# Four conditional layers on one core: the early expert blocks ordered by hand, their sums on two other engines, and two units of layer 3 moved

## The chip, the cores and the metric

One core of one Trainium2 chip. The time is the device time of one launch in microseconds (us). The engines are TensorE (PE, its weight loads shown as PEld), VectorE (DVE), ScalarE (ACT), GpSimd (POOL) and SyncE (SP); each runs its own instructions in order and waits on semaphores for the others.

## The reference, cut to what matters

Input x is 16 samples of 128 tokens by 128 columns. Each of four layers picks its weights by an index per sample or per token:

```python
# layer 0: one of 8 feed-forward networks per sample, then a layer norm
h = gelu(x @ Wi[i0] + bi[i0]); x = layernorm(h @ Wo[i0] + bo[i0] + x) * g[i0] + b[i0]
# layer 1: norm per token, norm over the tokens of a sample, scale and shift by a small network
h = norm_tokens(norm(x) * ln_g + ln_b) * gamma + beta
gates, idx = top_k(softmax(h @ router_w), 2)          # 2 of 8 experts per token
x = x + sum_over_the_two(gate * (relu(h @ w1[e] + b1[e]) @ w2[e] + b2[e]))
# layer 2: pairs of columns rotated by an angle per sample
# layer 3: down to 32 columns, gelu, a 32x32 expert per sample, up again, residual, layer norm
a = gelu(x @ down_W.T + down_b)
x = layernorm((a @ expert_W[i3].T + expert_b[i3] + emb[i3]) @ up_W.T + up_b + x) * g3 + b3
```

## The kernel before, in words

Layer 0 runs sample by sample on PE (`up`, `down`), in four groups of four samples. Groups 0 and 1 (half 0) are carried through layer 1's norm and router while groups 2 and 3 are still in layer 0.

Layer 1's experts work on blocks of 128 token rows that share an expert; there are NBLK = 39. A block's rows are fetched from a DRAM copy of h by an indirect DMA on POOL (`gather`, L536), transposed on PE (`rows_T`, L975) and copied to SBUF on ACT (`transposed`, L716); then PE multiplies by w1 (`blk_up`), ACT adds the bias and takes relu (`hidden`, L726), PE multiplies by w2 (`blk_down`), DVE adds the bias row b2 out of PSUM (`add_b2`, L1475), and POOL scatters the result to DRAM (`scatter`, L542). All PE matmuls go through the helper `mm` at L808. SP loads each block's w1 (`load_w1`, L440).

Which tokens belong to a block follows from the router: `top2`, a prefix count by matmul (`rank`), sorting on DVE (`ranks` to `sort_slots`), one-hot tiles (`hot_blocks` L1367, `hot_slots` L1374 on DVE, `hot_rows` L694 on ACT, `hot_tiles` L528 on POOL), a matmul with them (`inverse`) and `sources` (L1416 to L1421), which writes the gather's and scatter's indices. The first EARLY = 9 blocks are full blocks of half 0 and can start when half 0 is sorted. While they run, half 1 is normed (`l1_norm` on DVE), transposed (`z_transposes`), scaled (`row_stats`, `film_factors`, `film_h` L631), routed (`route`), ranked, sorted and stored to DRAM (`rows_back`, `store_rows` L639); these steps hang on block numbers in each engine's loop, as `if k == 5: route(3)`. Blocks 9 to 38 wait for `sources(1)` (semaphore v_idx at 2) and the stores of groups 2 and 3.

On POOL the order is written out: nine gathers with five `power` steps (L522) between them, `hot_tiles(1)`, scatters 0 to 3, `hot_tiles(2)`, then gathers 9 to 12, then in turn scatter n and gather n+9. On ACT a block's rows are transposed three steps before its `hidden`. On PE, downs run two blocks behind ups.

Layer 3 works on units of two samples. `scattered` and `load_y` (L446) on SP bring the expert outputs back; `combine` (L1484, L1492) on DVE adds them with their gates; PE transposes (`l3_T`, L1004), multiplies (`l3_down`, `l3_residual`, `l3_up`); ACT has `evac_uT` (L734), `gelu3` (L740), `norm3` (L749). Statistics are on DVE (`stats3` L1500 to L1505). Units 0 to 3 start in the block loop at step BEGIN3 = 30, take the square root on DVE by iteration (`root3`, L1511 to L1521) and finish there (`scale_shift3`, L1552 and L1556); units 4 to 7 follow once all blocks are scattered, with the root and the last scaling on POOL (`power3` L556, `gain_shift3` L548 and L552), the very last one on DVE (`last_norm`, L1537 and L1544). `store_out` (L460) writes a unit out.

## Time and profile before

| what | value |
|---|---|
| median of three runs | 231.68 us (230.59 to 233.28) |
| profiled execution: its own time, and the span of its instructions | 230.44 us, 228.6 us |
| mean granted PE clock | 0.842 of full speed |
| busy: PE, PEld, DVE, ACT, POOL | 178.3, 161.6, 116.6, 107.2, 109.0 us |

The profile is of one execution. Times in it count from the first instruction of the span. "Idle before" is the time in which an engine stood still ahead of an instruction, with what released it; "issue" means that it waited for nothing that the profile shows. The granted clock of PE is 1.00 at 2.4 GHz and 0.50 at 1.2 GHz.

### The profile page before, as it was taken

How to read it: one execution, taken by the hardware profiler on the slowest of the kernel's cores; microseconds unless marked ns; L12 is line 12 of the kernel's file. 1: busy time of each engine (PE TensorE's matmuls, PEld its weight loads, DVE VectorE, ACT ScalarE, POOL GpSimd, SP SyncE). 2: the span in 40 equal slices, each digit the busy share in tenths (PEclk: the TensorE clock that was granted, in tenths of full speed). 3: DMA queues.
4: the chain of work that ended last, by engine and by line, in shares of the span. 5: the costliest groups of instructions: out<-in, count | busy, mean ns of one | idle time of the engine just before them, and what ended most of it. 6: DMA issues, size and time to landing. Idle time of an engine off the chain costs nothing.

```text
span 228.6 us, 5312 instructions
## 1 busy us (share of the span) xinstructions
PE 178.3 (78%) x1287; PEld 161.6 (71%) x1287; DVE 116.6 (51%) x575; ACT 107.2 (47%) x338; POOL 109.0 (48%) x126
## 2 busy tenths in 40 slices
PE   6999997999959599284799888887799994077920
PEld 6999986898859599173798777876688873045710
DVE  6316798888943868940023343311236777353460
ACT  3564874665235566301566556564356651123310
POOL 5126335102870670127777777777776333101560
PEclk9999999997667859857589999999999999555555
DMA  6999999994643113047456565535951011330001
GB/s 205 294 322 337 329 317 301 250 292 123 220 130 100 26 34 106 1 104 231 137 154 186 156 173 146 147 97 173 319 167 57 26 46 47 106 134 1 26 25 44
DMA packets 35048, 34.82 MB, mean 152 GB/s; under 512 B 3793, under 2 KB 26475, under 8 KB 35019
## 3 DMA queue, kind: packets, MB, share of 16 engines
q1 hardware_dynamic: 27995, 26.56, 40.3%
q0 software_dynamic: 2496, 5.12, 7.5%
q10 hardware_dynamic: 4528, 2.81, 4.0%
q8 instruction: 12, 0.20, 0.4%
q14 instruction: 17, 0.14, 0.2%
HBM read 29.81 MB, written 4.65 MB: 151 GB/s over the span
## 4 chain that ended last, share of the span: by engine, by line
PE 35%; DVE 21%; POOL 19%; issue 11%; DMA 9%; DVEq 2%; ACT 1%; ACTq 0%; POOLq 0%; SPq 0%
PE bank L808 31%; POOL got L536 7%; POOL token_rows L542 7%; DMA got<-h_rows,src_i 6%; DVE st L1196 3%; PE bank L975 1%; POOL rstd L522 1%; DVE hot_in L1374 1%; POOL rs L556 1%; DVEq L1598 1%; DMA token_rows<-y_blk,dst_i 1%; DMA w_place<-token_rows 1%; DVE y_blk L1475 1%; DVE top_i L1272 1%; PE bank L1004 1%
## 5 line engine op out<-in xcount | busy, mean ns | idle before, releaser
L726 ACT ACTIVATE hid<-bank,small 128x128 f32<-128x128 f32 x156 | 44.4, 368 | 28.0 <-PE bank L808 27.2
L808 PE MATMUL bank<-w,hid 128*128 x312 | 46.5, 297 | 5.3 <-DVE y_blk L1475 4.8
L542 POOL DMA_INDIRECT token_rows<-y_blk,dst_i x39 | 38.8, 995 | 23.0 <-DVE y_blk L1475 13.4
L536 POOL DMA_INDIRECT got<-h_rows,src_i x39 | 38.2, 981 | 22.2 <-issue 10.1
L808 PE MATMUL bank<-gotT,w_now 128*128 128x128 f32 x312 | 46.8, 299 | 0.0
L808 PEld LDWEIGHTS bank<-w,hid 128*128 128x128 f32 x312 | 42.1, 209 | 6.3 <-issue 6.0
L808 PEld LDWEIGHTS bank<-gotT,w_now 128*128 128x128 f32 x312 | 42.9, 213 | 0.0
L1475 DVE TENSOR_TENSOR y_blk<-bank,b_tab 128x128 f32<-128x128 f32 x39 | 11.4, 291 | 58.5 <-PE bank L808 57.0
L975 PE MATMUL bank<-ident,got 128*128 128x128 f32 x39 | 13.0, 334 | 18.0 <-DMA got<-h_rows,src_i 13.2
L716 ACT ACTIVATE gotT<-bank 128x128 f32<-128x128 f32 x39 | 11.0, 282 | 27.2 <-PE bank L975 26.9
L667 ACT ACTIVATE act<-bank,small 128x128 f32<-128x128 f32 x64 | 18.0, 374 | 11.9 <-PE bank L808 11.5
L522 POOL TENSOR_TENSOR rstd<-veps,minus_half 128x4 f32<-128x4 f32 x12 | 12.3, 1027 | 20.9 <-DVE veps L1244 9.1
L975 PEld LDWEIGHTS bank<-ident,got 128*128 128x128 f32 x39 | 6.2, 160 | 22.4 <-DMA got<-h_rows,src_i 16.9
L808 PE MATMUL bank<-w_place,act 128*128 128x128 f32 x128 | 17.5, 279 | 0.7 <-ACT act L667 0.7
L808 PE MATMUL bank<-xT,w_place 128*128 128x128 f32 x128 | 17.1, 276 | 0.0
L808 PEld LDWEIGHTS bank<-w_place,act 128*128 128x128 f32 x128 | 15.5, 192 | 1.0 <-ACT act L667 0.9
L808 PEld LDWEIGHTS bank<-xT,w_place 128*128 128x128 f32 x128 | 15.6, 192 | 0.1
L1004 PE MATMUL bank<-ident,xbT 128*128 128x128 f32 x16 | 4.5, 372 | 10.7 <-DVE xbT L1492 10.7
L556 POOL TENSOR_TENSOR rs<-ve,minus_half 128x2 f32<-128x2 f32 x4 | 2.9, 714 | 18.6 <-DVE ve L1505 18.6
L1004 PEld LDWEIGHTS bank<-ident,xbT 128*128 128x128 f32 x16 | 2.3, 167 | 11.9 <-DVE xbT L1492 11.2
L749 ACT ACTIVATE zg<-bank,nmr,rs 128x128 f32<-128x128 f32 x14 | 5.6, 453 | 9.8 <-DVE nmr L1530 9.8
L808 PE MATMUL bank<-ident 128*128 128x128 f32 x38 | 8.4, 399 | 1.9 <-POOL minus_half L496 1.9
(232 smaller groups left out, 267.8 us busy)
## 6 DMA issues: line engine op xcount, KB each, us to landing
w_now<-in_exp_w SPq DMA_DIRECT2D x39, 256.0 KB, 3.3
w_place<-in_l_wi SPq DMA_DIRECT2D x16, 256.0 KB, 5.2
w_place<-in_l_wo SPq DMA_DIRECT2D x16, 256.0 KB, 5.6
rows<-in_l_rows SPq DMA_DIRECT2D x16, 128.0 KB, 4.9
w<-in_exp_w SPq DMA_DIRECT2D x8, 256.0 KB, 5.8
w_place<-token_rows SPq DMA_DIRECT2D x8, 256.0 KB, 3.5
x_sb<-in_x ACTq DMA_DIRECT2D x4, 256.0 KB, 4.5
h_rows<-h_row ACTq DMA_DIRECT2D x4, 256.0 KB, 2.8
```

The source lines that it names most:

```text
L522: g_.tensor_tensor(rstd[:, kind, g % 2, :], veps[:, kind, g % 2, :], minus_half[:], ALU.pow)\
L536: g_.indirect_dma_start(got[:, n % RING, :], None, h_dram[0:(HB if n < EARLY else NB) * P], bass.IndirectOffsetOnAxis(ap=src_i[:, n:n + 1] ...
L542: g_.indirect_dma_start(y_dram, bass.IndirectOffsetOnAxis(ap=dst_i[:, n:n + 1], axis=0), y_blk[:, n % YRING, :], None).then_inc(st_y[n % Y ...
L667: last = a_.activation(act0[:, b % 2, c, :], up_bank(b)[:, c * P:(c + 1) * P], ACT.Gelu, bias=cols[:, bass.ds(e * FC + (R_BI + c), 1)])
L716: a_.activation(gotT[:, n % TRING, :], got_bank, ACT.Copy).then_inc(a_gT, 1)
L726: last = a_.activation(hid[:, n % HRING, c, :], up_bank(n)[:, c * P:(c + 1) * P], ACT.Relu, bias=cols[:, bass.ds(e * FC + (R_B1 + c), 1)])
L749: last = a_.activation(z3[:, i, :], o3_bank[u][:, k * P:(k + 1) * P], ACT.Identity, bias=nmr3[:, i:i + 1], scale=rs3[:, i:i + 1])
L808: return t_.matmul(out_, lhsT, rhs, start=start, stop=stop)
L975: t_.transpose(got_bank, got[:, n % RING, :], ident[:]).then_inc(p_gT, 1)
L1004: last = t_.transpose(uT_bank[u][:, k * P:(k + 1) * P], u_b[:, place(u) + k, :], ident[:])
L1196: do(v_.bn_stats(st[:, kind, g % 2, k, :], src(k)))
L1475: v_.tensor_tensor(y_blk[:, n % YRING, :], y_bank(n), b2_tab[:, bass.ds(e, 1), :].rearrange("p o d -> p (o d)"), ALU.add)\
```

## The change

- The order of PE and ACT for the nine early blocks is written out. ACT transposes a block's rows at the block's own step instead of three before; PE interleaves the transposes of rows with ups, and the steps of half 1 stand between them at new places. The eight warming matmuls (`keep_warm(8, ...)`) are gone, and `experts3(2)`, `experts3(3)` and their evacuations move behind the early blocks.
- DVE no longer adds b2 for the early blocks. ACT copies the result out of PSUM (`evac_y`), and POOL adds b2 just before it scatters the block. DVE runs half 1's steps in one line, without additions between them.
- The z tiles of groups 2 and 3 are made on ACT (`norm1`), from a scaled mean that DVE writes (`minus_mean`).
- `hot_slots` makes its 16 tiles in two instructions with broadcast operands instead of 16; the slot numbers are bf16.
- Group 0 and 1 are stored at steps 13 and 14 of layer 0's loop. POOL scatters blocks 0 to 2 before `hot_tiles(2)` and block 3 after it. The y ring has 10 places instead of 12.
- BEGIN3 is 34: units 2 and 3 of layer 3 end behind the loop. Only unit 0 has its root on DVE; units 1 to 5 take `power3` and, but for their store, `gain_shift3` on POOL; units 6 and 7 end on DVE (`own_norm`). Value loads for `l3_up` are issued earlier (`l3_which`). `load_y` of the first units is two blocks later, and of the stores only unit 0's stands before the last reload.

The diff, cut to its core:

```diff
-    RING, YRING, TRING, WRING, HRING = 16, 12, 4, 6, 3
+    RING, YRING, TRING, WRING, HRING = 16, 10, 4, 6, 3
+    FIRST_OUT = 3
-    BEGIN3 = 30
+    BEGIN3 = 34
 # SP
-                if n == SETTLED + WRING + 2:
+                if n == SETTLED + WRING + 4:
...
-            for u in range(HU):
-                store_out(u)
+            store_out(0)
             scattered(NBLK)
             for u in range(HU, NU):
                 load_y(u)
-            for u in range(HU, NU):
+            for u in range(1, NU):
                 store_out(u)
 # GpSimd
             def scatter(n):
-                pool.wait_ge(v_y, n + 1)
+                if n < EARLY:
+                    pool.wait_ge(a_y, n + 1)
+                    e = pool.value_load(exp_i[0:1, n:n + 1], min_val=0, max_val=E1 - 1)
+                    ch.do(g_.tensor_tensor(y_blk[:, n, :], y_blk[:, n, :],
+                                           b2_tab[:, bass.ds(e, 1), :].rearrange("p o d -> p (o d)"), ALU.add))
+                    ch.settle()
+                else:
+                    pool.wait_ge(v_y, n - EARLY + 1)
...
-            for n in range(HELD):
+            pool.wait_ge(l_w2, 16 * (E1 + 1))
+            for n in range(FIRST_OUT):
                 scatter(n)
             hot_tiles(2)
+            for n in range(FIRST_OUT, HELD):
+                scatter(n)
...
+            power3(1)
+            power3(2)
+            gain_shift3(1)
+            gain_shift3(2)
+            power3(3)
+            gain_shift3(3)
             power3(HU)
...
 # ScalarE
-                if b == 14:
-                    store_rows(0)
+                if b >= 13 and b < 13 + HG:
+                    store_rows(b - 13)
...
+            for k in range(EARLY):
+                transposed(k)
+                if k == 2:
+                    norm1(2)
+                if k == 3:
+                    norm1(3)
+                if k == 5:
+                    film_h(2)
+                    film_h(3)
+                hidden(k, block_expert(k))
+                if k >= BEHIND:
+                    evac_y(k - BEHIND)
+                if k == 6:
+                    store_rows(2)
+                if k == 7:
+                    store_rows(3)
+                    hot_rows(1)
+            evac_y(EARLY - 2)
+            evac_y(EARLY - 1)
+            hot_rows(2)
+            evac_m3(2)
+            evac_m3(3)
+            transposed(EARLY)
+            transposed(EARLY + 1)
 # TensorE
-            experts3(2)
-            experts3(3)
             pe.wait_ge(v_bias, 1)
-            keep_warm(8, bank[6], ident[:])
...
+            rows_T(0)
+            blk_up(0)
+            rows_T(1)
+            blk_up(1)
+            rows_T(2)
+            pe.wait_ge(v_l0, NG)
+            blk_up(2)
+            down_of(0)
+            rows_T(3)
+            z_transposes(2)
+            blk_up(3)
+            down_of(1)
+            rows_T(4)
+            z_transposes(3)
+            blk_up(4)
+            down_of(2)
+            rows_T(5)
+            blk_up(5)
+            down_of(3)
+            rows_T(6)
+            route(2)
+            blk_up(6)
+            route(3)
+            down_of(4)
+            rows_T(7)
+            rank(1)
+            rows_back(2)
+            blk_up(7)
+            down_of(5)
+            rows_T(8)
+            rows_back(3)
+            blk_up(8)
+            down_of(6)
+            inverse(1)
+            down_of(7)
+            down_of(8)
+            experts3(2)
+            inverse(2)
+            experts3(3)
+            pe.wait_ge(v_exp, 2)
+            rows_T(EARLY)
+            rows_T(EARLY + 1)
+            for k in range(EARLY, NBLK + BEHIND):
...
+            l3_which(HU - 1)
+            l3_down(HU - 1)
+            l3_residual(HU - 1)
+            l3_up(HU - 1)
+            l3_which(HU)
+            l3_which(HU + 1)
             l3_T(HU)
             l3_T(HU + 1)
 # VectorE
             def hot_slots(h, first, past):
-                for j in range(first, past):
-                    last = v_.tensor_scalar(hot_in[:, h, j, :], col_bf[:], in_blk[:, j:j + 1], None, ALU.is_equal)
-                    if j % 4 == 3:
-                        last.then_inc(v_hot, 1)
+                n = past - first
+                v_.tensor_tensor(hot_in[:, h, first:past, :],
+                                 col_bf[:].rearrange("p (o n) -> p o n", o=1).to_broadcast([P, n, P]),
+                                 in_blk_bf[:, first:past].rearrange("p (j o) -> p j o", o=1).to_broadcast([P, n, P]),
+                                 ALU.is_equal).then_inc(v_hot, 1)
...
+                if u == 2 and odd == 0:
+                    stats3(0)
+                    root3(0)
+                    shift_of_norm3(0)
+            combine(HU - 1, unit(HU - 1))
+            scale_shift3(0)
+            stats3(1)
+            stats3(2)
+            shift_of_norm3(1)
+            shift_of_norm3(2)
             combine(HU, unit(HU))
+            stats3(3)
             combine(HU + 1, unit(HU + 1))
+            shift_of_norm3(3)
             combine(HU + 2, unit(HU + 2))
```

## Rows read from the trace of the kernel before

**Rows 1.** The page's first part: busy us, share of the span, instructions.
```profile
PE 178.3 (78%) x1287; PEld 161.6 (71%) x1287; DVE 116.6 (51%) x575; ACT 107.2 (47%) x338; POOL 109.0 (48%) x126
```

**Rows 2.** Chain of waits in order of time: start us, us, what.
```profile
62.06 3.50 DMA got<-h_rows,src_i
...
101.35 1.00 POOL got L536
...
194.51 0.30 DVE y_blk L1475
195.08 2.73 DMA token_rows<-y_blk,dst_i
197.94 2.56 DMA w_place<-token_rows
200.51 0.41 DVE z L1484 x2
```

**Rows 3.** Timeline of PE: start us, us, engine, line, what, count, idle before.
```profile
65.87 1.91 PE L808 MATMUL bank<-gotT,w_now 128*128 128x128 f32 x8
67.58 0.42 PE L975 MATMUL bank<-ident,got 128*128 128x128 f32 x1
...
72.22 1.06 PE L808 MATMUL bank<-gotT,w_now 128*128 128x128 f32 x8
...
87.89 0.20 PE L808 MATMUL bank<-both,behind 128*128 128x64 bf16 x1 [0.24 <-DVE both L1280]
...
178.21 0.27 PE L975 MATMUL bank<-ident,got 128*128 128x128 f32 x1
...
188.63 2.44 PE L808 MATMUL bank<-w,hid 128*128 x16 [0.34 <-issue]
...
210.90 1.22 PE L808 MATMUL bank<-m,a 33*128 x4 [0.87 <-issue]
```

**Rows 4.** Stretches: us, busy us (count) of PE, PEld, DVE, ACT, POOL, then PEclk, DMA, GB/s.
```profile
54.00:61.00 7.00, 7.00 (x38) 6.06 (x35) 6.66 (x36) 1.92 (x5) 4.42 (x5) 0.51 0.59 184
72.00:77.00 5.00, 4.07 (x37) 3.87 (x35) 4.03 (x25) 1.31 (x5) 2.55 (x3) 1.00 0.05 13
88.00:95.00 7.00, 4.73 (x54) 4.53 (x52) 5.86 (x26) 4.00 (x12) 0.98 (x1) 1.00 0.17 52
96.00:101.00 5.00, 3.46 (x27) 3.40 (x28) 3.14 (x16) 0.00 (x0) 0.00 (x0) 0.50 0.16 51
196.00:221.00 25.00, 15.63 (x56) 10.96 (x56) 10.70 (x43) 5.70 (x14) 6.29 (x10) 0.50 0.21 67
```

**Rows 5.** Timeline of POOL, columns as in group 3.
```profile
55.66 1.20 POOL L536 DMA_INDIRECT got<-h_rows,src_i  x1 [4.81 <-DMA h_rows<-h_row]
...
59.37 1.01 POOL L536 DMA_INDIRECT got<-h_rows,src_i  x1 [0.19 <-issue]
...
172.53 0.97 POOL L536 DMA_INDIRECT got<-h_rows,src_i  x1 [0.30 <-PE bank L975]
```

**Rows 6.** Timeline of ACT, columns as in group 3.
```profile
67.94 1.14 ACT L726 ACTIVATE hid<-bank,small 128x128 f32<-128x128 f32 x4 [1.55 <-PE bank L808]
...
77.49 1.50 ACT L631 ACTIVATE hT<-bank,film 128x128 f32<-128x128 f32 x4 [2.76 <-DVE film L1262]
...
81.40 0.95 ACT L694 ACTIVATE hot_blk<-hot_tmp,pair_no 128x240 bf16<-128x240 bf16 x2
...
88.63 0.60 ACT L639 ACTIVATE h_row<-bank 128x512 f32<-128x512 f32 x1 [0.38 <-PE bank L894]
```

**Rows 7.** Groups by line on POOL and DVE: count, busy us, mean ns, idle before.
```profile
L516 POOL TENSOR_TENSOR xbT<-xT,bo_cols 128x512 f32<-128x512 f32 x4 | 4.3, 1068 | 8.5 <-ACT xT L623 4.9 <-DVE hyp_a L1163 3.6
...
L548 POOL TENSOR_TENSOR zg<-zg,rows 128x256 f32<-128x256 f32 x3 | 2.2, 726 | 0.0
...
L1544 DVE SCALAR_TENSOR_TENSOR z<-zg,rs,rows 128x128 f32<-128x128 f32 x2 | 1.6, 844 | 0.3 <-POOL rs L556 0.3
```

**Rows 8.** Timeline of DVE after an `add_b2`, columns as in group 3.
```profile
74.98 0.89 DVE L1196 BATCH_NORM_STATS2 st<-bank 128x6 f32<-128x128 f32 x4 [0.37 <-issue]
```

More of the change, by code:

```diff
@@ L698, in _ @@
             hot_rows(0)
-            store_rows(1)
             def evac_m3(i):
@@ L705, in _ @@
             a_.activation(warm[:, 2, :], ones_row[:], ACT.Exp).then_inc(ac, 1)
-            for i in range(NG):
-                evac_m3(i)
+            evac_m3(0)
+            evac_m3(1)
             for i in range(E3, MT):
@@ L744, in norm3 @@
                 act.wait_ge(v_nmr3, u + 1)
-                if earlier(u) is not None:
-                    act.wait_ge(v_o3, earlier(u) + 1)
+                if earlier(u) == 0:
+                    act.wait_ge(v_o3, 1)
+                elif earlier(u) is not None:
+                    act.wait_ge(g_o3, earlier(u))
                 for k in unit(u):
@@ L751, in norm3, with norm1, evac_y @@
                 last.then_inc(a_z3, 1)
-            act.wait_ge(v_exp, 1)
-            transposed(0)
-            transposed(1)
-            e = block_expert(0)
-            for k in range(NBLK):
-                if k == EARLY:
-                    transposed(k)
-                    transposed(k + 1)
+            def norm1(g):
+                act.wait_ge(v_nmr1, g - HG + 1)
+                act.wait_ge(p_zT, g - 1)
+                for k in range(GS):
+                    last = a_.activation(z1[:, g % 2, k, :], x1[:, GS * g + k, :], ACT.Identity,
+                                         bias=nmr1[:, g % 2, k:k + 1], scale=rstd[:, 1, g % 2, k:k + 1])
+                last.then_inc(a_z1, 1)
+            def evac_y(n):
+                act.wait_ge(p_y, n + 1)
+                a_.activation(y_blk[:, n, :], y_bank(n), ACT.Copy).then_inc(a_y, 1)
+            act.wait_ge(v_exp, 1)
+            for k in range(EARLY):
[22 more added lines that the diff above has]
+            transposed(EARLY + 1)
+            act.wait_ge(v_exp, 2)
+            e = block_expert(EARLY)
+            for k in range(EARLY, NBLK):
                 hidden(k, e)
-                if k + 1 == EARLY:
-                    hot_rows(2)
-                    act.wait_ge(v_exp, 2)
                 if k + 1 < NBLK:
@@ L768, in _ @@
                     transposed(n)
-                if k == 3:
-                    film_h(2)
-                if k == 4:
-                    film_h(3)
-                    hot_rows(1)
-                if k == 5:
-                    store_rows(2)
-                if k == 6:
-                    store_rows(3)
                 if k == 12:
@@ L787, in _ @@
                     gelu3(u)
-                if 2 <= u and odd == 0:
-                    norm3(u - 2)
-            norm3(HU - 1)
+                if k == NBLK - 1:
+                    norm3(0)
+            gelu3(2)
+            evac_uT(3)
+            gelu3(3)
+            norm3(1)
+            norm3(2)
             evac_uT(HU)
+            norm3(3)
             evac_uT(HU + 1)
@@ L1022, in l3_residual, with l3_which @@
                 last.then_inc(p_res3, 1)
+            place3 = {}
+            def l3_which(u):
+                b, _ = UNITS[u]
+                place3[u] = [pe.value_load(m_idx[0:1, b + k:b + k + 1], min_val=0, max_val=MT - 1) for k in unit(u)]
             def l3_up(u):
                 b, n = UNITS[u]
-                which = [pe.value_load(m_idx[0:1, b + k:b + k + 1], min_val=0, max_val=MT - 1) for k in unit(u)]
+                which = place3.pop(u)
                 pe.wait_ge(a_gelu3, u + 1)
@@ L1043, in down_of @@
                 blk_down(n, e)
-            for k in range(NBLK + BEHIND):
-                if k == EARLY:
-                    down_of(k - 2)
-                    inverse(2)
-                    down_of(k - 1)
-                    pe.wait_ge(v_exp, 2)
-                    rows_T(k)
-                    rows_T(k + 1)
+            pe.wait_ge(v_exp, 1)
+            pe.wait_ge(a_gelu, NB)
+            pe.wait_ge(a_m3, 2)
+            rows_T(0)
[41 more added lines that the diff above has]
+            for k in range(EARLY, NBLK + BEHIND):
+                u, odd = divmod(k - BEGIN3, 2)
                 if k < NBLK:
                     blk_up(k)
-                if k >= BEHIND and k not in (EARLY, EARLY + 1):
+                if 1 <= u and odd == 0:
+                    l3_which(u - 1)
+                if k >= EARLY + BEHIND:
                     down_of(k - BEHIND)
@@ L1058, in _ @@
                     rows_T(n)
-                if k == 2:
-                    z_transposes(2)
-                    z_transposes(3)
-                if k == 4:
-                    route(2)
-                if k == 5:
-                    route(3)
-                    rows_back(2)
-                if k == 6:
-                    rank(1)
-                    rows_back(3)
-                if k == 7:
-                    inverse(1)
-                u, odd = divmod(k - BEGIN3, 2)
                 if k == BEGIN3:
@@ L1078, in _ @@
                     pe.wait_ge(v_midx, 1)
-                if 1 <= u <= HU and odd == 0:
+                if 1 <= u and odd == 0:
                     l3_up(u - 1)
@@ L1590, in _ @@
             l0_spread_shift(3)
+            minus_mean(2)
             l1_stats(3)
-            l1_norm(2)
-            l1_norm(3)
+            hot_blocks(1)
+            minus_mean(3)
+            later_bases()
+            row_stats(2)
+            row_stats(3)
+            film_factors(2)
+            film_factors(3)
+            part_experts()
+            top2(2)
+            top2(3)
+            ranks(1)
+            more_blocks()
+            sort_slots(1)
+            hot_blocks(2)
+            hot_slots(1, 0, KT // 2)
@@ L1634, in _ @@
+            dve.wait_ge(v_exp, 2)
+            e = b2_of(EARLY)
+            for k in range(EARLY + 1, NBLK + 1):
+                add_b2(k - 1, e)
+                if k < NBLK:
+                    e = b2_of(k)
                 if k == 14:
```

135 lines of the change are left out of this document (52 added, 83 removed).

## The prediction

> **What bounds the kernel now.** I read the page first, then the chain of waits in order of time, then the timelines of POOL, PE, ACT and DVE around the stretches that the chain names, the stretches' granted clock, and last the groups by line for prices. The page shows no engine full over the span [rows 1], so the stages have to be read one by one. Three stretches matter.
>
> First, the early blocks (55 to 101 us): nine expert blocks run while the second half of the batch is routed, and what ends them is the first late gather at 101.35 us [rows 2]. It waits for `sources(1)`, behind the routing chain: z transposes, film, logits, top2, `rank(1)` on PE at 87.89 us [rows 3], sorting, `inverse(2)`. TensorE moves between its two clock levels here: 1.2 GHz (0.51) from 54 to 61 us, where PE ran the 32-row matmuls of `experts3` and then the eight warming ones, 2.4 GHz from 72 to 77 and mostly from 88 to 95, and 1.2 again from 96 to 101, after PE had stood still for the sorting [rows 4].
>
> Second, the late blocks: from 101.35 to gather 38 at 172.53 us POOL issues back to back, gather and scatter in turn with 0.30 us between them [rows 2, 5]. That is 4 gathers and 26 pairs in 71.2 us, and PE, which needs less than 2 us a block at 2.4 GHz, waits for it. So POOL is the bound, and whatever is laid on POOL after 101 us is paid in full.
>
> Third, the end: gather 38 is used by PE at 178.21 us only, because two units of layer 3 stand before it; the last two downs start at 188.63 [rows 3] and end at 191.07, the last addition starts 3.4 us later, at 194.51, since DVE is busy with the square roots of layer 3; then scatter, reload and the first combine at 200.51 [rows 2].
>
> **The change part by part.** All is summed against the profiled execution, 230.44 us (span 228.6 us).
>
> *A, the start of gather 9.* `store_rows(1)` moves from behind `hot_rows(0)` to step 14, so gather 0, which waited for that store [rows 5], waits for `src_i` instead: about 54.6 for 55.66 us. It lands 3.5 us later (as the gather at 62.06 did [rows 2]), and the first block is transposed at 58.1. The eight warming matmuls are gone, so I take PE at 1.2 GHz there: an up or a down holds PE for 67.58 - 65.87 = 1.71 us at that level; its eight matmuls take 1.91 with their tail there and 1.06 at the other level, where it is 0.89 by the same subtraction [rows 3]. In the new order ACT transposes block k only after `hidden(k-1)`, so a block is a round trip: up 1.71, hand-over and drain about 0.35, `hidden` about 1.0 [rows 6], two more short steps 0.4, together 3.5 us. `up(2)` begins at 65.7, and with one up, one down and a transpose z goes through at 69.4. At 2.4 GHz from there `z_transposes(3)` follows at 71.8. A full-speed block is then 0.89 + 0.89 + about 1.1 of drain, evacuation and transposition on ACT, 2.9 us. `up(5)` is at 75.9; ACT then runs two `film_h` of 1.4 us each (start to next start about 1.4, by the 1.50 of the row [rows 6]), `hidden(5)`, one evacuation and `transposed(6)` before PE can start `up(6)` at 80.1; `route(3)` and top2 (0.9, 0.8 and 1.8 us with `up(6)` and the hand-over) put `rank(1)` at 83.6; with one group at the lower level 84.4, 3.5 us earlier than now.
>
> From `rank(1)` to gather 9 the path is now 13.46 us. In the new order it holds six PE groups (the ups of blocks 7 and 8, the downs of 5 to 8) and four half groups (two `rows_back`, two inverses), 8 x 0.89 = 7.1 us at full clock and 8 x 1.71 = 13.7 at half; ACT steps: two stores with their DMA issues (2 x 1.0 by the store's row), two `hot_rows` of 0.95, three short copies, 4.7 us; `sources` 0.65; nine hand-overs at about 0.27, 2.4 us. Sum 14.9 at full clock, 21.5 at half. The removed DVE additions and the one-hot tiles in two instructions lie beside this, since ACT's `evac_y(8)` and `hot_rows(2)` are now the last before `inverse(2)`. I take a third of the stretch at the lower level, as the 5 us before 101 are now [rows 4]: 17.1. Then gather 9 starts at 101.5, 0.15 later than now: **0 us**, between -2.3 (no half clock after `rank(1)`) and +4.4 (half clock throughout).
>
> The Trainium skill's page TensorE: Matmul & The Clock Gate (Part 1, and HAM oscillation) says that the slow level is the default and that PE idling brings it back; the trace agrees, with 0.50 after the idle sorting [rows 4]. By that rule the round trips speak against the change; the third rival below is its case.
>
> *B, five additions on POOL.* Blocks 0 to 2 and 3 are added and scattered before gather 9, in time POOL spends waiting; blocks 4 to 8 come after it, in the stretch that POOL bounds. Each gets a register load, a 128x128 addition and a wait, and loses one 0.30 us gap. No row has this addition: 128x256 takes 726 ns and 128x512 takes 1068 [rows 7], and a line through them gives 0.55 us at 128. A load costs 0.33 of the 0.37 us that DVE idles after each add [rows 8]. After an arithmetic instruction the next DMA comes 0.19 us later [rows 5]. With 0.03 between instructions: 0.03 + 0.33 + 0.55 + 0.19 - 0.30 = 0.80, five times: **+4.0 us**. From below: half of 726 and a hidden load, 0.28 each, 1.4 us. From above: 0.73 and the longest idle for loads on PE, 0.87 [rows 3], 1.52 each, 7.6 us.
>
> By the Trainium skill's GPSIMD Engine Reference (3.1 Elementwise) a two-input operation costs some 2.6 cycles an element; an estimate by that page takes 0.28 from the 0.73 of 256 columns and puts the addition at 0.45, half a microsecond less in all.
>
> *C, the end.* With unit 0 and 1 begun four steps later, PE meets gather 38 as it lands, about 3.0 us after issue instead of the 5.7 of now (178.21 - 172.53): -2.7. From there to the end of the last down it now takes 12.9 us; the new order lays one transposition, one down and one residual more before it: +0.6 by the same rows' rates. DVE has one root there instead of four, done before the last addition: -3.1 of the 3.4. Scatter and reload (2.73 and 2.56 [rows 2]) stay; `store_out(0)` stands before the reload on SP, but DVE is done with its unit about as the scatter lands. In the tail PE is at 1.2 GHz [rows 4]; unit 3's residual and up stand before unit 4's transposes, 2 x 1.22 = +2.4; the 0.87 us of loads before `up(5)` go [rows 3]; the last norm, 844 ns a piece beside a busy POOL [rows 7] against some 350 alone, saves 0.9. Tail +0.6. Sum of C: -2.7 + 0.6 - 3.1 + 0.6 = **-4.6 us**, between -6.5 and -2 (tail order).
>
> The other edits (value loads ahead, the m3 evacuations moved behind the early blocks, ring of 10, later reload) I put at nothing: PE's queue or POOL's bound covers them; uncovered, each is under 1 us.
>
> Sum: 0 + 4.0 - 4.6 = -0.6: 229.8 us on the profiled execution's scale. The runs' median, 231.68, is 1.24 above that execution; for a median I add half of it, 0.6: 230.4, and as much to the rivals' times below. The forecast is no change that can be told (1%, 2.3 us, is about what a measurement of this kernel tells from none).
>
> **The rivals.** *TensorE stays at 2.4 GHz after `rank(1)`*: A is -2.3, the sum -2.9, 228.1. For it: 88 to 95 is full now. Against it: the drop at 96.
>
> *The additions cost little*: B is 1.4, the sum -3.2, 227.8. For it: POOL's queue may load ahead. Against it: each `settle` stops it.
>
> *The early stage runs at 1.2 GHz* (slower): between `rank(1)` and gather 9 PE waits for ACT at each block, the clock falls and stays; A +4.4, the sum +3.8, 234.8. It decides once gather 9 starts later than 104.2 us (-0.6 + 2.9 = 2.3). For it: `inverse(2)` now hangs on the last down through ACT. Against it: at half clock PE is dense, and dense work brought the clock back by 72 us.
>
> *The last addition isn't freed*: DVE's combine, first statistics and root3 in step 36 hold it; -3.1 becomes 0, the sum +2.5, 233.5. Against it: these are 4.6 us, and two further steps of PE (5 us) lie behind them.
>
> **How the numbers follow.** Forecast 0.41, full clock 0.20, cheap additions 0.14, half clock 0.20, held addition 0.05. Faster by over 1%: 0.34; within: 0.41; slower: 0.25. The range goes from below the two faster cases together (-4.4 at worst) to the slower one: 226.0 to 235.0; the likeliest case alone, 228.5 to 232.5.
>
> **What would show it.** Gather 9 within 99 to 104 us with `rank(1)` some 3 to 4 us earlier than now; about 0.8 us more from gather to scatter for blocks 4 to 8 and 2.56 us a pair after; gather 38 near 177; no idle between the last down and the last addition; clock rows of 0.5 between 90 and 101. Wrong if gather 9 comes before 98 us, or if POOL waits between its DMAs in the late stretch.

## The result, and the profile after

The change makes the kernel slower by 1%: 232.13 us median against 230.44 us, 22 runs each, ratio 1.0095 (95% interval 1.0064 to 1.0126). Timed a second time beside the experiments it came to 1.0125 (1.0073 to 1.0176). A ratio is taken over the executions that count as undisturbed (15 of these 22 of the changed kernel, two of six of the run with the early stage alone), so it can differ a little from the quotient of the medians beside it.

The first profile after is of a long execution (237.04 us, span 235.0). A second one, taken with the experiments, is of 232.26 us (span 230.4), near the median, and stands beside it. Milestones, us from the start of the span:

| milestone | before | forecast | after, near the median | after, long |
|---|---|---|---|---|
| first `route` of half 0 | 38.91 | | 40.66 | 39.59 |
| gather 0 | 55.66 | 54.6 | 56.88 | 57.38 |
| `rank(1)` | 87.89 | 84.4 | 86.35 | 88.73 |
| gather 9 (A) | 101.35 | 101.5 | 103.62 | 108.33 |
| first `route` to gather 9 | 62.44 | 62.6 | 62.96 (+0.52) | 68.74 (+6.30) |
| gather 9 to 38 (B) | 71.18 | +4.0 | 73.28 (+2.10) | 73.26 (+2.08) |
| gather 38 to first combine of unit 4 (C) | 27.98 | -5.2 | 25.65 (-2.33) | 25.60 (-2.38) |
| from there to the end (C) | 28.09 | +0.6 | 27.85 (-0.24) | 27.81 (-0.28) |
| span | 228.6 | | 230.4 | 235.0 |

From gather 9 on, the columns of before and after add up to their spans; near the median the differences are +2.27 + 2.10 - 2.33 - 0.24 = +1.80. The two executions of the changed kernel differ only before gather 9.

Of the +2.27 at gather 9 near the median, 1.75 us is not the change's. The first `route` stands ahead of every step that the change moved, and it already came 1.75 us later. The delay arises from 7 to 11 us: PE's first groups of eight take 2.08 and 1.82 us there instead of 1.16 and 1.06. In the trace of before the granted clock rises to its full level at 6.4 us, in this one at 10.6. (In the long execution it rises at 5.4; its first `route` is 0.68 late after PE had waited 0.95 us for a weight load.) Before, then near the median:

```profile
6.84 1.16 PE L808 MATMUL bank<-ident 128*128 128x128 f32 x8
...
38.91 0.96 PE L808 MATMUL bank<-small,hT 128*128 128x8 f32 x8
```

```profile
7.09 2.08 PE L851 MATMUL bank<-ident 128*128 128x128 f32 x8
8.96 1.82 PE L851 MATMUL bank<-xT,w_place 128*128 128x128 f32 x8
...
40.66 0.96 PE L851 MATMUL bank<-small,hT 128*128 128x8 f32 x8
```

So the early stage is best measured from the first `route`. Two further profiles below share the changed early order on PE and ACT, and they took 66.40 us (early stage alone) and 67.97 us (additions left out) from there to gather 9. Of the four, the one near the median has the shortest early stage.

Busy times (they answer to [rows 1]) and the clock granted to PE in 40 slices, page of the long execution, then the clock of the other:

```profile
PE 183.0 (78%) x1271; PEld 162.8 (69%) x1271; DVE 106.6 (45%) x496; ACT 111.6 (48%) x353; POOL 121.6 (52%) x142
...
PEclk9999999998557965569569999999999999555555
```

```profile
PEclk9999999999557997787589999999999999555555
```

PE is busy for about as long as before; POOL has 12.6 us more. The clock digits of slices 15 to 18 (82 to 106 us, and 81 to 104 us in the shorter span) differ between the two: 6, 5, 5, 6 in the long one, 9, 7, 7, 8 in the other.

POOL in the long execution, which answers to [rows 5]:

```profile
57.38 1.20 POOL L538 DMA_INDIRECT got<-h_rows,src_i  x1 [4.50 <-DMA h_rows<-h_row]
...
108.33 0.97 POOL L538 DMA_INDIRECT got<-h_rows,src_i  x1 [9.62 <-DVE src_i L1506]
...
115.14 0.96 POOL L538 DMA_INDIRECT got<-h_rows,src_i  x1 [0.30 <-issue]
116.12 0.46 POOL L546 TENSOR_TENSOR y_blk<-y_blk,b_tab 128x128 f32<-128x128 f32 x1
116.86 1.00 POOL L551 DMA_INDIRECT token_rows<-y_blk,dst_i  x1 [0.28 <-POOL y_blk L546]
118.17 0.96 POOL L538 DMA_INDIRECT got<-h_rows,src_i  x1 [0.30 <-issue]
...
181.59 0.96 POOL L538 DMA_INDIRECT got<-h_rows,src_i  x1 [0.30 <-issue]
```

A pair with an addition takes 118.17 - 115.14 = 3.03 us (2.56 without). Gather 0 still waits for the store here; the chain of waits shows that store taking 8.28 us:

```profile
48.20 8.28 DMA h_rows<-h_row
57.38 3.73 DMA got<-h_rows,src_i
```

POOL in the other execution, same places:

```profile
56.88 1.20 POOL L538 DMA_INDIRECT got<-h_rows,src_i  x1 [2.92 <-DVE src_i L1506]
...
103.62 0.97 POOL L538 DMA_INDIRECT got<-h_rows,src_i  x1 [7.38 <-DVE src_i L1506]
...
176.90 0.96 POOL L538 DMA_INDIRECT got<-h_rows,src_i  x1 [0.31 <-issue]
```

PE there, which answers to [rows 3]: three ups that wait for `gotT`, `rank(1)` at 86.35, the transposition of block 38 at 180.03, and at the end the residual of unit 2 and the last down.

```profile
82.77 1.16 PE L851 MATMUL bank<-gotT,w_now 128*128 128x128 f32 x8 [1.13 <-ACT gotT L733]
...
86.35 0.20 PE L851 MATMUL bank<-both,behind 128*128 128x64 bf16 x1 [0.52 <-DVE both L1364]
...
88.51 1.59 PE L851 MATMUL bank<-gotT,w_now 128*128 128x128 f32 x8 [1.46 <-ACT gotT L733]
89.90 1.91 PE L851 MATMUL bank<-w,hid 128*128 x8
...
94.92 1.21 PE L851 MATMUL bank<-gotT,w_now 128*128 128x128 f32 x8 [2.17 <-ACT gotT L733]
...
180.03 0.27 PE L1020 MATMUL bank<-ident,got 128*128 128x128 f32 x1
...
192.44 0.71 PE L851 MATMUL bank<-x_sb,xT 128*128 128x128 f32 x4 [0.34 <-ACT zg L768]
...
194.60 1.83 PE L851 MATMUL bank<-w,hid 128*128 x8 [1.44 <-issue]
```

Why the ups wait shows on ACT: `transposed(8)` (94.61) stands behind the second store and `hot_rows(1)`, and only then can PE do `up(8)` at 94.92.

```profile
92.78 0.60 ACT L657 ACTIVATE h_row<-bank 128x512 f32<-128x512 f32 x1 [0.66 <-PE bank L940]
93.41 0.37 ACTq L659 DMA_DIRECT2D h_rows<-h_row  x1
93.83 0.88 ACT L712 ACTIVATE hot_blk<-hot_tmp,pair_no 128x240 bf16<-128x240 bf16 x2 [0.45 <-ACT h_row L657]
94.61 0.25 ACT L733 ACTIVATE gotT<-bank 128x128 f32<-128x128 f32 x1
```

Granted clock by stretches, columns as in [rows 4], the long execution and then the other:

```profile
84.00:88.00 4.00, 4.00 (x21) 4.00 (x20) 2.17 (x20) 1.14 (x4) 3.05 (x5) 0.50 0.12 37
96.00:100.00 4.00, 1.83 (x9) 1.57 (x8) 2.26 (x4) 1.64 (x4) 2.43 (x3) 0.50 0.27 82
```

```profile
84.00:88.00 4.00, 2.53 (x22) 2.05 (x21) 2.92 (x23) 2.02 (x6) 2.46 (x3) 1.00 0.12 37
88.00:92.00 4.00, 3.49 (x18) 3.49 (x19) 3.62 (x16) 1.57 (x6) 0.32 (x1) 0.63 0.25 70
96.00:100.00 4.00, 4.00 (x35) 3.94 (x35) 0.00 (x0) 1.42 (x5) 0.24 (x1) 0.59 0.55 150
```

In the long execution PE runs at 1.2 GHz (0.50) from 84 to past 100 us; in the other the stretch is mixed. In both, PE had waited 1.1 to 1.2 us for ACT ahead of `up(6)` and 1.46 ahead of `up(7)`.

### The profile page after: what moved, and what is told of

Same layout as the page of the kernel before. It is cut to its first block, busy times and chain, and to the rows that moved or that the text cites. A ratio compares the mean times of both kernels' runs of the same rounds, so it can differ in the third digit from the quotient of the medians.

```text
span 235.0 us, 5235 instructions
## 1 busy us (share of the span) xinstructions
PE 183.0 (78%) x1271; PEld 162.8 (69%) x1271; DVE 106.6 (45%) x496; ACT 111.6 (48%) x353; POOL 121.6 (52%) x142
## 4 chain that ended last, share of the span: by engine, by line
PE 25%; POOL 23%; issue 18%; DMA 15%; DVE 7%; ACT 5%; ACTq 1%; POOLq 1%; SPq 1%; DVEq 0%
PE bank L851 22%; POOL got L538 11%; POOL token_rows L551 9%; DMA got<-h_rows,src_i 5%; DMA h_rows<-h_row 4%; DMA w_place<-in_l_wi 2%; ACT hid L743 1%; DMA w_place<-token_rows 1%; DVE st L1277 1%; DVE xbT L1577 1%; DMA ids<-in_ids 1%; DMA token_rows<-y_blk,dst_i 1%; PE bank L940 1%; POOL rs L566 1%; PE bank L1020 1%
## 5 line engine op out<-in xcount | busy, mean ns | idle before, releaser
L851 PE MATMUL bank<-gotT,w_now 128*128 128x128 f32 x312 | 50.0, 312 | 8.8 <-ACT gotT L733 7.5
L851 PEld LDWEIGHTS bank<-gotT,w_now 128*128 128x128 f32 x312 | 44.9, 222 | 11.3 <-ACT gotT L733 9.5
L851 PE MATMUL bank<-w,hid 128*128 x312 | 47.6, 302 | 1.6 <-issue 1.5
L851 PEld LDWEIGHTS bank<-w,hid 128*128 128x128 f32 x312 | 43.1, 214 | 2.7 <-issue 2.3
L1560 DVE TENSOR_TENSOR y_blk<-bank,b_tab 128x128 f32<-128x128 f32 x30 | 8.8, 292 | 65.5 <-PE bank L851 62.1
L1020 PE MATMUL bank<-ident,got 128*128 128x128 f32 x39 | 13.5, 345 | 22.6 <-DMA got<-h_rows,src_i 18.6
L1277 DVE BATCH_NORM_STATS2 st<-bank 128x6 f32<-128x128 f32 x32 | 7.1, 283 | 9.2 <-PE bank L923 6.0
L530 POOL TENSOR_TENSOR hot_blk<-hot_tmp,col_bf 128x480 bf16<-128x480 bf16 (+1 forms) x3 | 4.2, 1411 | 13.4 <-DVE hot_tmp L1451 13.4
L566 POOL TENSOR_TENSOR rs<-ve,minus_half 128x2 f32<-128x2 f32 x7 | 5.0, 715 | 10.5 <-DVE ve L1590 10.4
L851 PE MATMUL bank<-x_sb,xT 128*128 128x128 f32 x32 | 8.3, 401 | 1.6 <-ACT zg L768 1.6
L851 PEld LDWEIGHTS bank<-x_sb,xT 128*128 128x128 f32 x32 | 6.2, 273 | 4.2 <-ACT zg L768 2.3
```

The source lines that it names most:

```text
L530: g_.tensor_tensor(hot_blk[s][:, :, 1, :].rearrange("p (k t) n -> p k t n", k=TOPK), hot_tmp[s][:].rearrange("p (k t) n -> p k t n", k=TOP ...
L566: g_.tensor_tensor(rs3[:, there(u)], ve3[:, there(u)], minus_half[:, 0:UNITS[u][1]], ALU.pow)\
L851: return t_.matmul(out_, lhsT, rhs, start=start, stop=stop)
L1020: t_.transpose(got_bank, got[:, n % RING, :], ident[:]).then_inc(p_gT, 1)
L1277: do(v_.bn_stats(st[:, kind, g % 2, k, :], src(k)))
L1560: v_.tensor_tensor(y_blk[:, n % YRING, :], y_bank(n), b2_tab[:, bass.ds(e, 1), :].rearrange("p o d -> p (o d)"), ALU.add)\
```

## The experiments

Times of before in them are medians of 11 to 23 runs, 230.1 to 230.9 us. The diffs are cut to their core.

**The end alone, the early stage alone.** First the kernel before with the change's end (`BEGIN3 = 34` and all that follows the blocks):

```diff
-    BEGIN3 = 30
+    BEGIN3 = 34
...
-            for u in range(HU):
-                store_out(u)
+            store_out(0)
```

> The kernel before with the change's end alone: layer 3 begun at step 34, units 2 and 3 behind the loop, roots on GpSimd, own_norm, the new order of stores. The early blocks are those of before. Theory (the early stage loses what the end gains): in the changed kernel's profile the stretch from gather 38's issue to the first combine of unit 4 was 25.6 us against 28.0, and the tail 0.3 us shorter, so the end alone gives -2.7 us, a ratio of 0.988 (0.984 to 0.992). Rival 1 (the end gives all of the forecast 4.6): 0.980. Rival 2 (the last addition is still held, the end gives nothing): 0.998 to 1.003.

226.65 us, ratio 0.9861 (0.9792 to 0.9930). Gathers 9 and 38 come when they came before, and unit 4's first combine at 197.56 us instead of 200.51 [rows 2]:

```profile
101.19 1.00 POOL L535 DMA_INDIRECT got<-h_rows,src_i  x1 [6.48 <-DVE src_i L1449]
...
172.37 0.99 POOL L535 DMA_INDIRECT got<-h_rows,src_i  x1 [0.30 <-issue]
```

The end alone gains, 172.37 to 197.56 = 25.2 us for 27.98; the theory's size fits, the forecast's (0.980) lies inside the interval too, and "gives nothing" falls. The tail is 0.55 us shorter as well.

The reverse, the changed early stage with the end of before:

```diff
-    BEGIN3 = 34
+    BEGIN3 = 30
...
-            store_out(0)
+            for u in range(HU):
+                store_out(u)
```

> The changed kernel with the end of before (layer 3 begun at step 30, roots on VectorE, stores and last norm as before); the early blocks are the changed ones. Theory: the early stage costs what is missing, +1.0% and the 2.7 us of the end, some +4.9 us, a ratio of 1.021 (1.015 to 1.030), with gather 9 at 103 to 108 us against 101.35. Rival 1 (only the five additions on GpSimd cost, gather 9 comes when it did): +2.4 us, 1.010, gather 9 at 101 to 102. Rival 2 (the early stage costs nothing and the loss is in the end): 1.000.

239.24 us, ratio 1.0303 (1.0173 to 1.0432): slower, at the edge of the theory's range. All six runs (234.84 to 240.28) are longer than all 17 of before beside them (227.49 to 231.91), but the size is poorly known. Gather 9 is at 107.13 and the way to gather 38 takes 73.9 us:

```profile
107.13 0.98 POOL L539 DMA_INDIRECT got<-h_rows,src_i  x1 [8.32 <-DVE src_i L1479]
...
180.98 0.96 POOL L539 DMA_INDIRECT got<-h_rows,src_i  x1 [0.30 <-issue]
```

So the loss is in the early stage and its POOL additions, not in the end.

**The additions left out.**

```diff
                 if n < EARLY:
                     pool.wait_ge(a_y, n + 1)
-                    e = pool.value_load(exp_i[0:1, n:n + 1], min_val=0, max_val=E1 - 1)
-                    ch.do(g_.tensor_tensor(y_blk[:, n, :], y_blk[:, n, :],
-                                           b2_tab[:, bass.ds(e, 1), :].rearrange("p o d -> p (o d)"), ALU.add))
-                    ch.settle()
```

> The changed kernel with the b2 additions and their register loads on GpSimd left out for blocks 0 to 8, so those rows lack b2. Theory: five of them lie in the stretch that GpSimd bounds, 3.03 us a gather-scatter pair against 2.56, 0.47 each; leaving them out gives -2.4 us, so 0.999 of the kernel before (0.995 to 1.003). Rival 1 (each costs the forecast 0.80): -4.0 us, 0.992. Rival 2 (GpSimd does not set the end, the additions are hidden): as the changed kernel, 1.0095.

231.11 us, ratio 0.9994 (0.9940 to 1.0048), as the theory had it; gather 9 to 38 is 177.68 - 106.85 = 70.83 us, 2.45 less than the changed kernel's 73.28. The additions cost 0.47 to 0.49 us each, not 0.80.

```profile
106.85 0.98 POOL L538 DMA_INDIRECT got<-h_rows,src_i  x1 [8.60 <-DVE src_i L1502]
...
177.68 0.96 POOL L538 DMA_INDIRECT got<-h_rows,src_i  x1 [0.30 <-issue]
```

**Blocks transposed one ahead.** On PE `rows_T(k+1)` moves before `blk_up(k)`, on ACT `transposed(k+1)` before `hidden(k)`, for blocks 1 to 8 (ACT's part):

```diff
+            transposed(0)
             for k in range(EARLY):
-                transposed(k)
+                if k + 1 < EARLY:
+                    transposed(k + 1)
                 if k == 2:
                     norm1(2)
```

> The changed kernel with each early block's rows transposed one block ahead, on TensorE and on ScalarE: transposed(k+1) stands before hidden(k), so an up no longer waits for the chain hidden, transposed. Theory (these round trips hold the early stage): the idle times before the ups (0.43, 1.30, 1.34, 0.68, 1.20, 1.46 and 2.17 us in the profile, ScalarE's gotT) go, gather 9 comes 3 to 5 us earlier, ratio 0.990 to 0.997 of the kernel before. Rival (the routing chain on VectorE and ScalarE and the granted clock set gather 9, the ups only fill its waits): gather 9 within 1 us of the changed kernel's, ratio 1.006 to 1.013.

224.10 us, ratio 0.9797 (0.9730 to 0.9863): the round trips were the cost, and more of it than expected. `rank(1)` is at 83.98 and gather 9 at 95.97 us, 7.7 earlier than in the changed kernel's execution near the median, though the first `route` (41.12) was even later than there; from it to gather 9 it takes 54.85 us, 8.1 to 13.9 less than in the four profiles above. The granted clock is 0.97 to 1.00 from 66 us until gather 9:

```profile
95.97 0.97 POOL L538 DMA_INDIRECT got<-h_rows,src_i  x1 [2.08 <-DVE src_i L1508]
```

```profile
66.00:72.00 6.00, 5.13 (x43) 4.79 (x42) 2.71 (x18) 5.48 (x20) 2.38 (x2) 0.97 0.54 170
84.00:88.00 4.00, 4.00 (x38) 4.00 (x39) 3.31 (x17) 2.32 (x8) 0.69 (x1) 1.00 0.29 86
88.00:95.00 7.00, 5.18 (x64) 4.29 (x63) 5.33 (x10) 4.27 (x13) 4.28 (x3) 1.00 0.16 47
```

**Which round trips.** Only blocks 1 to 5 ahead, then only 6 to 8 (`AHEAD = (6, 7, 8)`), on PE likewise:

```diff
+            AHEAD = (1, 2, 3, 4, 5)
             for k in range(EARLY):
-                transposed(k)
+                if k not in AHEAD:
+                    transposed(k)
+                if k + 1 in AHEAD:
+                    transposed(k + 1)
```

> The changed kernel with only blocks 1 to 5 transposed one block ahead; blocks 6 to 8 as in the change. With all of 1 to 8 ahead, gather 9 came at 95.97 us for 108.33, 4.8 of it before the rank matmul (83.98 for 88.73) and 7.6 between that and gather 9. Theory (both halves of the early stage lose by round trips, each its own part): the rank matmul at 84 to 85.5 us, the way from there to gather 9 still 17 to 19, gather 9 at 102 to 103.5, ratio 0.990 to 1.000. Rival (only the late trips count, since the rank matmul hangs on film and top2): the rank matmul stays at 88 to 89, ratio 1.005 to 1.013.

230.01 us. The ratio, 1.0096 (1.0005 to 1.0186), lies in the rival's stretch and not in the theory's, but the medians are equal (230.09 before) and 2 to 3 us under those of the changed kernel, so the times decide nothing. The profile is of the shortest of the twelve executions (226.25 us), and there `rank(1)` came at 81.99, not at the 88 to 89 of the rival: from gather 0 to `rank(1)` it takes 81.99 - 55.56 = 26.4 us for 29.5, from there to gather 9 still 16.6, with `up(8)` waiting 2.17 us as before:

```profile
81.99 0.23 PE L855 MATMUL bank<-both,behind 128*128 128x64 bf16 x1
...
89.85 1.46 PE L855 MATMUL bank<-gotT,w_now 128*128 128x128 f32 x8 [2.17 <-ACT gotT L733]
```

> The changed kernel with only blocks 6 to 8 transposed one block ahead, so that ScalarE no longer holds these behind the two films, the two stores and hot_rows. Theory: the rank matmul stays near 88.7 us, from there to gather 9 it takes 12 to 13.5 us instead of 18 to 19.6, gather 9 at 101 to 102, ratio 0.982 to 0.992. Rival (what was gained behind the rank matmul came only from a clock that the earlier blocks had raised): still 17 us or more, ratio 1.003 to 1.012.

226.59 us, ratio 0.9860 (0.9804 to 0.9915). From `rank(1)` to gather 9 it is 98.45 - 86.46 = 12.0 us for 17.3, as the theory had it; `up(8)` waits for nothing and takes 1.06 us.

```profile
86.46 0.20 PE L855 MATMUL bank<-both,behind 128*128 128x64 bf16 x1 [1.09 <-DVE both L1368]
...
89.22 1.06 PE L855 MATMUL bank<-gotT,w_now 128*128 128x128 f32 x8
```

So the larger part is ACT's order behind `rank(1)`: blocks 7 and 8 were transposed behind the two stores and `hot_rows(1)`. PE is at full clock there too (1.00 from 84 to 100 us), so order and clock come together in this run.

**The clock by itself.** The changed order, with warming matmuls where PE waits:

```diff
+            pe.wait_ge(a_hid, 5)
+            keep_warm(3, up_bank(6), ident[:])
             route(2)
+            keep_warm(4, up_bank(6), ident[:])
...
+            pe.wait_ge(a_hid, 6)
+            keep_warm(5, up_bank(7), ident[:])
             blk_up(7)
...
+            pe.wait_ge(a_hid, 7)
+            keep_warm(7, up_bank(8), ident[:])
             blk_up(8)
```

> The changed kernel with its order kept, and warming matmuls of 128x128 on TensorE in its waits after block 5: three before route(2), four behind it, five behind rows_back(2), seven behind rows_back(3). Theory (the round trips cost by themselves and also by the lower clock): the granted clock stays near 1.0 to 95 us or beyond, an up or a down takes 1.06 us instead of 1.9 to 2.1, six of those and the halves behind the rank matmul give 4 to 5 us back of the 7.6, gather 9 at 102.5 to 104.5, ratio 0.988 to 0.998. Rival 1 (only the order of ScalarE counts, TensorE's clock is not on the path): gather 9 at 106.5 or later, ratio 1.005 to 1.020. Rival 2 (only the clock counts): gather 9 at 101 or earlier, ratio under 0.985.

229.47 us, ratio 0.9970 (0.9926 to 1.0014; one of its twelve runs took 870.61 us and is not in the ratio), as the theory had it. PE holds 2.4 GHz from 78 to 100 us, with ACT's order unchanged, and gather 9 comes at 101.92 us, 0.6 before the theory's stretch:

```profile
88.00:95.00 7.00, 6.03 (x50) 5.47 (x48) 6.52 (x20) 3.60 (x11) 2.63 (x2) 1.00 0.26 75
95.00:101.00 6.00, 5.65 (x69) 4.90 (x68) 1.49 (x4) 3.16 (x10) 1.65 (x2) 1.00 0.39 105
```

From `rank(1)` (87.02) to gather 9 that is 14.9 us. With the order also mended it is 12.0; in the four profiles of the changed order 17.3, 17.9, 18.3 and, at half clock, 19.6. So the order costs up to 2.9 us there (the warming matmuls' own time is in the 14.9) and the clock 2.4 to 4.7 more, by execution.

**Additions of blocks 4 to 8 on DVE.** Blocks ahead, and behind `sources(1)`:

```diff
             dve.wait_ge(v_exp, 2)
+            for n in range(HELD, EARLY):
+                e = b2_of(n)
+                dve.wait_ge(a_y, n + 1)
+                v_.tensor_tensor(y_blk[:, n, :], y_blk[:, n, :],
+                                 b2_tab[:, bass.ds(e, 1), :].rearrange("p o d -> p (o d)"), ALU.add).then_inc(v_y, 1)
```

> All early blocks transposed one ahead (as in the run at 0.980), and the additions of blocks 4 to 8 moved from GpSimd to VectorE, behind sources(1), from SBUF to SBUF; GpSimd then only scatters these. Theory: the five pairs take 2.56 us again for 3.03, -2.4 us, ratio 0.969 (0.966 to 0.974). Rival (VectorE and GpSimd hold each other up, or VectorE's additions come too late for the scatters): -1 us or less, 0.975 to 0.985.

221.06 us, ratio 0.9622 (0.9570 to 0.9674), a little better than the theory: by the medians 3.0 us less than with the blocks ahead alone. Gather 9 to 38 is 166.24 - 95.47 = 70.8 us, about as before the change (71.18).

**The changed kernel again**, for the second profile shown above:

> The changed kernel unaltered, for a second profile beside the others, since its first was of an execution of 237.04 us, 4.9 above its median. Theory (a low clock behind the rank matmul makes gather 9 late, by an amount that differs between executions): in an execution near the median gather 9 is at 105 to 107.5 us for 108.33, with TensorE's granted clock near 0.5 to 0.6 between 92 and 105, the rest of the trace as in the first profile; ratio 1.005 to 1.015. Rival (the first profile shows the usual early stage, and long executions are long elsewhere): gather 9 at 108 or later.

233.07 us, ratio 1.0125 (1.0073 to 1.0176). In the profiled execution of 232.26 us gather 9 was at 103.62, earlier than the theory's 105 to 107.5, and the clock was 0.63 between 88 and 92 but 0.93 from 92 to 96. The direction holds (the long execution is long only before gather 9), its size near the median was set too high from the one long profile. And 1.75 of these 103.62 us come from the first 11 us, as shown above, which the theory did not think of.

**The register loads before the last down.** In the kernel with additions on DVE:

```diff
+                if k == NBLK:
+                    down_of(k - BEHIND)
+                    l3_which(u)
+                    last_e = pe.value_load(exp_i[0:1, NBLK - 1:NBLK], min_val=0, max_val=E1 - 1)
+                elif k > NBLK:
+                    blk_down(NBLK - 1, last_e)
```

> The kernel of the run at 0.962 (blocks transposed ahead, additions of blocks 4 to 8 on VectorE), and at the end TensorE's three register loads ahead of the last down moved one step up, before the residual of unit 2 that waits for norm3(0). Theory (of the forecast 4.6 us at the end some 1.5 are lost in these loads, 1.43 to 1.48 us of idle time before the last down): the last down starts 1.2 to 1.5 us earlier, -1.2 us, ratio 0.957. Rival (the loads are not on the path: the last addition is held by VectorE or the scatter queue): the idle time goes or moves, the time stays, 0.960 to 0.964.

219.18 us, ratio 0.9485 (0.9436 to 0.9534), better than the theory; by the medians -1.9 us. From gather 38 to unit 4's first combine it is 189.59 - 166.24 = 23.35 us against 25.04 without it. The loads' idle time (1.12) now lies beside the wait for `norm3(0)`, and the last down follows at once:

```profile
181.48 0.62 PE L853 MATMUL bank<-xT,dw_rot 128*32 128x128 f32 x4 [1.12 <-issue]
182.03 0.71 PE L853 MATMUL bank<-x_sb,xT 128*128 128x128 f32 x4
182.57 1.06 PE L853 MATMUL bank<-w,hid 128*128 x8
```

**The root of unit 0 on POOL**, on top of that:

```diff
+                if n == BEGIN3 + 1:
+                    power3(0)
...
                     stats3(0)
-                    root3(0)
+                if u == 2 and odd == 1:
                     shift_of_norm3(0)
```

> As the run with the loads one step up, and the square root of unit 0 of layer 3 on GpSimd (power3(0) behind scatter 35) instead of VectorE's eleven-step root. Theory (VectorE's root holds the addition of block 36 by some 2 us, and with it the down of block 38 and norm3(0), for which the residual of unit 2 waits 0.3 us): the last addition comes 1.5 to 2.5 us earlier, ratio 0.948 to 0.952. Rival (the root lies in a time in which the last downs wait for something else): no more than 0.3 us against the run with the loads alone.

220.46 us, ratio 0.9532 (0.9491 to 0.9573): no gain. The addition of block 36 came 1.9 us earlier, counted from gather 38, but the last addition did not (17.8 us behind gather 38, and 17.5 without this edit): the loads stand behind the down of block 37 in any case. DVE's root is not on the path.

**The first stores back at their places**, on the kernel with the loads moved:

```diff
-                if b >= 13 and b < 13 + HG:
-                    store_rows(b - 13)
+                if b == 14:
+                    store_rows(0)
...
+            store_rows(1)
...
-                if b == 13:
+                if b == 14:
+                    rank(0)
                     rows_back(0)
-                if b == 14:
+                if b == 15:
                     rows_back(1)
-                    rank(0)
```

> The kernel of the run at 0.949 with the first stores at their places of before: rows_back(0) behind the rank matmul, rows_back(1) a step later, store_rows(0) at step 14 and store_rows(1) behind hot_rows(0). Theory (the moved rows_back delays the rank matmul by 0.45 us, 7.00 to 7.44 from the first route, and the store that was issued 3.3 to 4 us earlier lands no earlier beside the weight loads): gather 0 at 55.5 to 56.7 us for 57.0, the rank matmul of half 0 again 7.0 us behind the first route's start, gather 9 0.5 to 1.3 us earlier, ratio 0.943 to 0.947. Rival (the first stores' place does not matter, gather 0 differs between executions anyway): gather 0 near 57, ratio 0.947 to 0.952.

218.31 us, ratio 0.9436 (0.9395 to 0.9476), inside the theory's range, though the interval overlaps that of the run before it (0.9436 to 0.9534). The rank matmul of half 0 is again 46.33 - 39.32 = 7.0 us behind the first route (7.45 in the changed kernel), and gather 0 waits for its indices, not for the store:

```profile
39.32 0.96 PE L854 MATMUL bank<-small,hT 128*128 128x8 f32 x8
...
46.33 0.20 PE L854 MATMUL bank<-both,behind 128*128 128x64 bf16 x1 [0.16 <-DVE both L1373]
```

```profile
56.46 1.20 POOL L538 DMA_INDIRECT got<-h_rows,src_i  x1 [4.28 <-DVE src_i L1515]
```

Gather 9 (96.38) was not earlier in this profile, taken of an execution 2.1 us over the median. So the 0.45 us is shown, its worth in the end is not. This version has the lowest ratio of all, 5.6% under the kernel before, but it cannot be told from the one before it.

## Why the prediction was wrong

It forecast -0.6 us on the profile's scale; near the median it is +1.8, and the runs say 1.0 to 1.25% (2.2 to 2.9 us) slower. The step that failed is A, the start of gather 9, put at 0. B and C were both over-sized, by 1.9 and 2.0 us, and cancel by luck. Term by term:

- **What bounds the kernel**: right. Every stretch that POOL bounds kept its length but for the additions. From gather 9 to the end it takes 125.4 to 126.8 us in the changed kernel's two profiles and in the four that alter the order or the clock of its early blocks alone, so gather 9's start carries through.
- **A, gather 0**: wrong. The step said that with the earlier store gather 0 waits for `src_i`, at 54.6, a gain of 1.1. Near the median it came at 56.88, 2.3 later than forecast. Of that, 1.75 us come from the first 11 us of the execution, as shown with the result, and not from the change. The rest is the forecast's: `rows_back(0)` now stands ahead of the second route on PE and delays the rank matmul by 0.45 us; and 54.6 is when `src_i` begins to be written, while the gather starts 0.48 later. The way from the rank matmul to `src_i` was 0.4 shorter. In the long execution the store, issued 3.3 us earlier (48.20 for 51.48), took 8.28 us beside the weight loads. In six of the eleven profiles with the moved store, the long one among them, gather 0 still waited for it; in the others the indices were late. From the first `route`, gather 0 comes after 16.2 to 18.6 us in these eleven, for 16.75 before and 15.7 forecast: the gain is not there.
- **A, the round trips**: the mechanism right, one number for it wrong. From gather 0 to gather 9 the forecast took 46.9 us, a third of the last stretch at the lower clock. Near the median it was 46.7: 29.5 to `rank(1)` for 29.8, then 17.3 for 17.1. The three other profiles with this order took 49.4 to 51.0: 31.4 to 31.9, then 17.9 to 19.6. The waits for ACT are alike in all four. The granted clock is not: from 72 to 78 us the three others have 0.70 to 0.86 and the one near the median 1.00, from 84 to 88 it is 0.50 to 0.72 for 1.00, and from 88 to 92 it is 0.50 for 0.63. So over the whole early stage A is +0.5 us in one profile and +4.0 to +6.3 in three, where 0 was forecast. The full-clock sum of 14.9 was met by the run with PE kept warm (14.9), in part by luck, since that stretch holds the warming matmuls too. That the round trips are losses that another order of ACT avoids (12.0 us) was not seen: the ACT steps were summed, and not asked who stands behind them in the queue.
- **B**: over-sized. +4.0 forecast, +2.1 measured. The addition takes 0.46 us and not 0.55, the wait behind it 0.28 and not 0.19, and the load of 0.33 us lies beside the DMA issue. The estimate by the Trainium skill's page GPSIMD Engine Reference (3.1 Elementwise) was 0.45 for the addition; the trace agrees, with 0.46.
- **C**: the sign right, the size not: -2.6 for -4.6. Block 38 is transposed 3.13 us after its gather for 5.68, -2.55 for the -2.7 forecast; the last addition follows its down at once, -3.3 for -3.1; the tail is 0.24 shorter and not 0.6 longer. But from that transposition to the end of the last down it takes 16.4 us for 12.9, where +0.6 was forecast. Of the 2.9 us missed, 1.44 are the loads ahead of the last down (the run with the loads moved shows them on the path), 0.34 the residual's wait for `norm3(0)`, and 0.7 the size of the inserted steps themselves: the down and residual of unit 2 alone take 0.62 + 0.71 us. The last two downs take 0.4 more than before (0.99 + 1.83 us for 2.44), the last one at the lower clock.
- **The range and the median**: the two faster cases together come to -2.3 + 1.4 - 4.6 = -5.5 us, 225.5 us, so the -4.4 and 226.0 of the range do not cover them. And the 0.6 us added for a median had no ground: over 22 runs the median of before is 230.44, the profiled execution's own time.
- **The rivals**: "the early stage runs at 1.2 GHz" is what three of the four profiles show, the long one most of all (gather 9 at 108.33, 107.13 and 106.85, past the 104.2 from which it was to decide); near the median the kernel stops short of it. "The additions cost little" (0.28 each) came nearer to the 0.47 measured than the forecast's 0.80. "The last addition isn't freed" falls as stated, but a later down took some of the gain.

## What to carry to other kernels

When an engine's steps are put into one written-out order, ask of each short step that another engine waits for (here a copy of 0.28 us) what now stands ahead of it in the queue, and put it there as early as its input allows. A first transfer that is issued earlier into a busy DMA queue need not land earlier. And register loads behind a semaphore wait are on the path: three of them cost 1.44 us ahead of the last down, but only 0.24 between two running matmul groups (in the profile near the median an up at 181.33 holds PE for 0.89 us, and the down behind it starts at 182.46). When two profiles are compared, take the times from a step ahead of the change that both share, or a difference between executions passes for the change's.

## What the runs showed of the hardware that was not expected

- The changed kernel's times spread over 229.7 to 237.0 us in 22 runs (before: 227.5 to 233.3), and the longer ones have the lower mean granted clock: 0.824 in the run of 237.04, 0.875 in that of 229.72. In the five kernels with all blocks ahead six runs lie within 1.2 to 4.3 us (220.2 to 221.4 with the additions on DVE, 217.5 to 221.8 with the stores back).
- PE's granted clock first rises to the full level at 5.2 to 6.8 us in nine of the fourteen profiles and at 10.6 to 11.7 us in the other five, at instructions that are the same in all. The first `route` is at 38.8 to 39.6 us in the nine and at 40.7 to 41.1 in the five.
- In the long execution a store of one group issued at 48.2 us landed later than one issued at 51.5 us had in the kernel before (gather 0 at 57.38 and 55.66), while the weight loads held the DMA (289 GB/s from 48 to 51 us).
- The same 128x128 addition on POOL takes 0.46 us alone and 1.43 (96.00 to 97.43 us, long execution) while DVE makes the one-hot tiles (93.98 to 97.13).
